# The decay of the first half of the channels in SBUF, its PSUM bank given to the ring

## The chip, the cores and the metric

One Trainium2 chip, one core of it. The metric is device microseconds of one execution, as the median of several. The kernel is written out by hand for the five engines: TensorE (PE, with its weight loads as PEld), VectorE (DVE), ScalarE (ACT), GpSimd (POOL) and the queue of SyncE (SP) that issues the DMAs.

## What is computed

Two transformer layers with adaptive layer norms over x of 8 batches x 512 positions x 128 channels. Only the first stage of the first layer matters here. It mixes each batch twice, from the same normed input:

```python
# causal attention, 16 heads of 8 channels
scores = jnp.where(causal, einsum('bqhd,bkhd->bhqk', q, k) * hd ** (-0.5), -inf)
attn_out = einsum('bhqk,bkhd->bqhd', softmax(scores), v).reshape(B, L, Dm) @ o_w + o_b
# selective state space model, 256 channels (two halves of 128), 16 states
def step(h, inp):
    xt, dtt, Bt, Ct = inp
    h = jnp.exp(dtt[..., None] * A) * h + (xt * dtt)[..., None] * Bt[:, None, :]
    y = einsum('bn,bdn->bd', Ct, h)
x = x + alpha * attn_out + (1.0 - alpha) * ssm_out
```

Behind it come an ffn, a mixture of eight experts with a shared one, banded attention and a last gated layer.

## The kernel before, in words

A planner (`plan_mixers` and its like) writes one list of steps. Each engine's program goes through this list in order and does its own share of each step, so the order of the instructions of every engine is fixed when the kernel is built. Between engines stand semaphore waits (`wait_ge`). Each engine works its queue in order: an instruction that waits holds all that is behind it.

The first stage runs from about 120 us to 840 us of the span. Three strands are woven together by `run_together`: `attend` (scores, exponential, weighing of the values), `maxima` (the row maxima of the scores, two units ahead) and `mamba` (the state space model), in fixed proportions. The stage repeats itself for each of the 8 batches, about every 93 us.

The state space model goes over 128 groups g (8 batches x 16 states). A group has two halves h of 128 channels, and takes:

- `spread` (L1863, SP): a DMA that spreads one row of B over 128 partitions into Bb, four groups ahead.
- `weight` (L1760, POOL): dBx = dtx * Bb, two instructions, two groups ahead. The buffer dBx holds four groups.
- `decay` (L1628, ACT): exp(A * dt), two instructions. Half 0 is written to PSUM bank 4, half 1 to bank 5. There is one buffer for each half, so the decay of group g+1 waits until the scan of group g has read it.
- `scan` (L1325, DVE): h = decay * h + dBx along the 512 positions, two instructions. Each reads the decay (PSUM) and dBx (SBUF) and writes hst (part of the tile hy, SBUF).
- `accumulate` (L1177 PE, L1261 DVE, in some groups ACT L1635 and POOL L1765): one group behind.

PSUM has 8 banks. In this stage bank 3 collects the weighed values, banks 4 and 5 hold the decay, and the five banks 0, 1, 2, 6 and 7 are the `ring`. Every other product of TensorE takes a bank of the ring by `take()`, which calls `first_free`: it picks the bank that the planner's own estimates have free first. So do the maxima (PE L1050, read by DVE L1315 into Mx), the scores (PE L1050, read by ACT L1569 into PT, then cut to the causal part by POOL L1740), the transposed states of `accumulate`, the projections and the branches of the model. TensorE's step waits for the release of its bank by the engine that read it last (`free[f"b{k}"]`).

The tile On is 128 x 2 x 512 in SBUF. POOL writes the normalised attention of head group 1 into On[:, 0] and of group 3 into On[:, 1] (`on`, L1745), and TensorE reads it four pieces of attention later (`wo`, line 1130). At the very start of the kernel On[:, 0] also serves as scratch (gtmp), and the mixture of experts later uses rows 0 to 32 of it (hr).

Of the kernel before, what the change touches and what calls it, by code (L numbers as in the profile page):

```python
# [10 lines left out]
ALU = mybir.AluOpType  # L11
ACT = mybir.ActivationFunctionType
# [152 lines left out]
def plan_mixers(p, r_h, r_n, lnb):  # L165

    free, up, step = p.free, p.up, p.step
    ring = [0, 1, 2, 6, 7]
    r_parts, r_v, r_qk, r_mr = {}, {}, {}, {}
    h_last = [None] * NB  # L170
    late, later, pts = [], [], [0]
# [65 lines left out]
    def normalise(b, g, m):  # L237
        hf, k = g // 2, 3
        it = step("os", b=b, g=g, m=m, os_free=free.get("Os"))
        it["o"] = free[f"b{k}"] = up("act_os")  # L240
        o1 = it["o"]
        yield
        yield
        k = take()
        it = step("on", b=b, g=g, o1=o1, bank=k, free=free.get(f"b{k}"), lrs_free=free.get(f"lrs{hf}"), on_free=free.get(f"On{hf}"))
        it["m"] = up("pe_dn")
        it["e1"] = free[f"b{k}"] = up("act_dn")
        it["e2"] = up("act_dn")
        it["o"] = free["Os"] = free[f"lrs{hf}"] = on = up("pool_on")
        for _ in range(4):  # L250
            yield
        k = take()
        it = step("wo", b=b, g=g, bank=k, free=free.get(f"b{k}"), on=on, h=h_last[b] or r_n[b])
        it["m"] = free[f"On{hf}"] = up("pe_wo")
        it["hd"] = free.get("hd")
        it["x"] = free[f"b{k}"] = up("act_hd")
        it["y"] = free["hd"] = h_last[b] = up("pool_h")
# [109 lines left out]

    def decay(g):
        b, n = divmod(g, 16)
        it = step("decay", g=g, dt=ssm[b]["dt"], free=[free.get(f"b{4 + h}") for h in range(2)])  # L370
        it["x"] = ssm[b]["decay", n] = [up("act_da"), up("act_da")]
        if n == 15:
            free[f"dtv{b % 2}"] = it["x"][1]

    def scan(g):
        b, n = divmod(g, 16)
        it = step("scan", g=g, into=ssm[b]["in", n], decay=ssm[b]["decay", n], free=[free.get(f"hst{2 * (g % 3) + h}") for h in range(2)])
        it["x"] = ssm[b]["h", n] = [up("dve_scan"), up("dve_scan")]
        for h in range(2):
            free[f"b{4 + h}"] = free[f"dBx{g % 4}{h}"] = it["x"][h]  # L380

    def accumulate(g):
        b, n = divmod(g, 16)
# [101 lines left out]
    mixer = mamba()  # L485
    drain(project(0))
    fetch(0)
    for k in (0, 1, 2):
        ring.remove(k)
    run_together(p.norms(first_norms([(1, 1)] + [(b, l) for l in range(2) for b in range(2, NB)])), 12, (mixer, 5, False))  # L490
    ring.extend((0, 1, 2))
    fetch(1)
    run_together(maxima(0), 23, (chain(values_of(0), project(1)), 8, True), (mixer, OFF, False))
    tops = chain(*[maxima(u) for u in range(1, NU)])
# [354 lines left out]
def build(nc, d, out):  # L849
    with ExitStack() as ctx:  # L850
# [38 lines left out]
        cT = sb("cT", [P, 16])  # L889
        mod = sb("mod", [P, 2, 6, NB])  # L890
        gab = sb("gab", [P, 4, NB])
        gtmp = On[:, 0, 0:96].rearrange("p (i j b) -> p i j b", i=3, j=4)
        avec = sb("avec", [P, 4])
        lsq = sb("lsq", [P, 2, T])
# [151 lines left out]
        def tensor_program(engine):  # L1046
# [22 lines left out]
            for kind, it in p.steps:  # L1069
# [57 lines left out]
                    mm(o[:], seld[:], Os[:]).then_inc(sems["pe_dn"], 1)  # L1127
                elif kind == "wo":
                    q.wait_ge(("ld_wo", 128), it["on"], it["free"])
                    mm(o[:], wo[:, it["g"] // 2, :], On[:, it["g"] // 2, :]).then_inc(sems["pe_wo"], 1)  # L1130
                elif kind == "taps":
                    q.wait_ge(("ld_in", 16), it["free"])
                    for h in range(2):
# [123 lines left out]
        def vector_program(engine):  # L1257
# [37 lines left out]
            for kind, it in p.steps:  # L1295
# [25 lines left out]
                elif kind == "scan":  # L1321
                    g = it["g"]
                    for h in range(2):
                        q.wait_ge(it["into"][h], it["decay"][h], it["free"][h])
                        engine.tensor_tensor_scan(hst[:, 2 * (g % 3) + h, :], bank[4 + h][:], dBx[:, g % 4, h, :], 0.0,  # L1325
                                                  ALU.mult, ALU.add).then_inc(sems["dve_scan"], 1)
                elif kind == "acc" and it["g"] % 16 and not it["beside"]:
                    b, n = divmod(it["g"], 16)
# [186 lines left out]
        def scalar_program(engine):  # L1515
# [25 lines left out]
            for kind, it in p.steps:  # L1541
# [82 lines left out]
                elif kind == "decay":  # L1624
                    b, n = divmod(it["g"], 16)
                    for h in range(2):
                        q.wait_ge(("dve_set", dve_set["A"]), it["dt"][h], it["free"][h])
                        engine.activation(bank[4 + h][:], dtv[:, b % 2, h, :], ACT.Exp,  # L1628
                                          scale=alog[:, h, n:n + 1]).then_inc(sems["act_da"], 1)
                elif kind == "acc" and (it["g"] % 16 == 0 or it["beside"]):  # L1630
                    b, n = divmod(it["g"], 16)
# [56 lines left out]
        def gpsimd_program(engine):  # L1688
# [39 lines left out]
            for kind, it in p.steps:  # L1728
# [13 lines left out]
                elif kind == "on":  # L1742
                    hf = it["g"] // 2
                    q.wait_ge(it["e2"], it["on_free"])
                    engine.tensor_tensor(On[:, hf, :], Os[:], rdn[:, hf, :], ALU.mult).then_inc(sems["pool_on"], 1)  # L1745
                elif kind in ("wo", "so"):
                    t = hT[:, it["b"], :]
                    q.wait_ge(it["x"], it["h"])
                    engine.tensor_tensor(t, t, hd[:], ALU.add).then_inc(sems["pool_h"], 1)
                elif kind == "dt":  # L1750
                    h, s = it["h"], it["b"] % 2
                    q.wait_ge(it["a3"], it["v1"], it["dtv_free"])
                    engine.tensor_tensor(dtv[:, s, h, :], sp1[:, h, :], sp2[:, h, :], ALU.add).then_inc(sems["pool_dt"], 1)
                    q.wait_ge(it["v2"], it["dtx_free"])
                    engine.tensor_tensor(dtx[:, s, h, :], dtv[:, s, h, :], xc[:, s, h, :], ALU.mult).then_inc(sems["pool_dt"], 1)
                elif kind == "weight":
                    b, sl = it["g"] // 16, it["g"] % 4
                    for h in range(2):
                        q.wait_ge(it["dx"][h], it["row"], it["free"][h])
                        engine.tensor_tensor(dBx[:, sl, h], dtx[:, b % 2, h], Bb[:, sl], ALU.mult).then_inc(sems["pool_dbx"], 1)  # L1760
                elif kind == "acc" and it["beside"]:
                    j = 2 * it["half"]
                    t = yT[:, j:j + 2, :]
                    q.wait_ge(it["y"], it["y_last"])
                    engine.tensor_tensor(t, t, yB[:, j:j + 2, :], ALU.add).then_inc(sems["pool_y"], 1)  # L1765
                elif kind == "yt":
                    h, s = it["h"], it["b"] % 2
                    q.wait_ge(it["y2"], it["z"])
                    engine.tensor_tensor(zg[:, s, h, :], zg[:, s, h, :], xc[:, s, h, :], ALU.mult).then_inc(sems["pool_yz"], 1)
                elif kind == "wsplit":  # L1770
                    e, s1, s2 = it["e"], stage[:, 2 * (it["i"] % 3), :], stage[:, 2 * (it["i"] % 3) + 1, :].rearrange("p (k n) -> p k n", k=4)
                    q.wait_ge(it["x1"])
                    engine.tensor_tensor(we1l[:, e, :], s1, we1h[:, e, :].bitcast(F32), ALU.subtract).then_inc(sems["pool_ws"], 1)
                    q.wait_ge(it["x2"])
                    engine.tensor_tensor(we2l[:, e], s2, we2h[:, e].bitcast(F32), ALU.subtract).then_inc(sems["pool_ws"], 1)
                elif kind == "moe_const":
                    q.wait_ge(it["done"])
                    engine.iota(iot_i[:], pattern=[[-1, 8]], base=8, channel_multiplier=0).then_inc(sems["pool_mc"], 1)
                    q.wait_ge(("pool_mc", 1))
                    engine.tensor_copy(iot[:], iot_i[:]).then_inc(sems["pool_mc"], 1)  # L1780
                elif kind == "moe_end":
                    t = acc[:, it["b"] % 2, :]
                    q.wait_ge(it["x"], it["acc"])
                    engine.tensor_tensor(t, t, prd[:, it["e"] % 2, :], ALU.add).then_inc(sems["pool_acc"], 1)  # L1784
                elif kind == "sc4" and it["s"] not in ON_DVE:
                    r, s = it["rg"], it["s"]
                    q.wait_ge(it["ready"], it["free"], it["done"])
                    engine.tensor_tensor(prod[:, it["ps"]], qkv[:, r % 3, 0, s:s + 1, :].broadcast_to([P, 8, P]), qkv[:, r % 3, 1],  # L1788
                                         ALU.mult).then_inc(sems["pool_p4"], 1)
                elif kind == "w4" and it["s"] not in ON_DVE:  # L1790
                    r, s = it["rg"], it["s"]
                    pr4 = scs[:, r % 2, :, 8 * s:8 * s + 8].rearrange("p k (h o) -> p k h o", o=1).broadcast_to([P, 8, 8, 16])
                    q.wait_ge(it["y"], it["free"])
                    engine.tensor_tensor(prod[:, it["ps"]].rearrange("p k (h x) -> p k h x", x=16), pr4,  # L1794
                                         qkv[:, r % 3, 2].rearrange("p k (h x) -> p k h x", x=16), ALU.mult).then_inc(sems["pool_w4"], 1)
                elif kind == "keys5":
                    t = kk[:, it["b"] % 2, :]
                    q.wait_ge(it["k"])
                    engine.tensor_tensor(t, t, t, ALU.mult).then_inc(sems["pool_k5"], 1)
# [150 lines left out]
```

## Time and profile before

| what | value |
| --- | --- |
| median of 3 runs | 1673.72 us (1668.92 to 1680.34) |
| the profiled execution, its own time | 1669.76 us |
| span of its profile, first to last instruction | 1668.0 us |
| granted TensorE clock, mean over the span | 0.934 |
| DVE busy | 1261.6 us (76% of the span) |
| PE busy | 1408.5 us (84%) |
| ACT busy | 1093.5 us (66%) |
| POOL busy | 863.4 us (52%) |

The profile counts an instruction as busy from its start to its end, and the end can contain time in which it was held inside the engine. Idle time is put down to the semaphore event that ended it. The shares are means over the whole span, and the first stage differs from the rest.

### The profile page before, as it was taken

How to read it: one execution, taken by the hardware profiler on the slowest of the kernel's cores; microseconds unless marked ns; L12 is line 12 of the kernel's file. 1: busy time of each engine (PE TensorE's matmuls, PEld its weight loads, DVE VectorE, ACT ScalarE, POOL GpSimd, SP SyncE). 2: the span in 40 equal slices, each digit the busy share in tenths (PEclk: the TensorE clock that was granted, in tenths of full speed). 3: DMA queues.
4: the chain of work that ended last, by engine and by line, in shares of the span. 5: the costliest groups of instructions: out<-in, count | busy, mean ns of one | idle time of the engine just before them, and what ended most of it. 6: DMA issues, size and time to landing. Idle time of an engine off the chain costs nothing. (4 is left out here: it accounts for less than half of the span.)

```text
span 1668.0 us, 22123 instructions
## 1 busy us (share of the span) xinstructions
PE 1408.5 (84%) x7164; PEld 884.0 (53%) x7164; DVE 1261.6 (76%) x1873; ACT 1093.5 (66%) x1864; POOL 863.4 (52%) x889
## 2 busy tenths in 40 slices
PE   3688898888989898887767887999999999868687
PEld 3234444444444444444324645787786877725573
DVE  2149999989798988989915858687686767848857
ACT  2475668686767778786746736777878788621017
POOL 3137677778696978878843113022222222248843
PEclk9787899999999999999988989999999999979889
DMA  3112222222222222222003010111111111000001
GB/s 90 45 39 83 77 63 78 80 75 70 64 68 67 78 73 68 80 76 75 27 1 95 19 48 26 33 48 45 40 49 39 45 45 45 26 0 1 0 1 50
DMA packets 61688, 84.73 MB, mean 51 GB/s; under 512 B 6621, under 2 KB 32071, under 8 KB 61575
## 3 DMA queue, kind: packets, MB, share of 16 engines
q1 hardware_dynamic: 61474, 83.30, 16.0%
q8 instruction: 58, 0.95, 0.2%
q14 instruction: 56, 0.45, 0.1%
q10 hardware_dynamic: 100, 0.03, 0.0%
HBM read 74.38 MB, written 8.78 MB: 50 GB/s over the span
## 5 line engine op out<-in xcount | busy, mean ns | idle before, releaser
L1760 POOL TENSOR_TENSOR dBx<-dtx,Bb 128x512 f32<-128x512 f32 x256 | 319.6, 1272 | 11.4 <-DMA Bb<-b_dram 10.1
L1355 DVE TENSOR_TENSOR hl<-lsq,hh 128x512 fp32r<-128x512 f32 x320 | 259.5, 821 | 86.7 <-ACT hh L1644 78.9
L1325 DVE TENSOR_TENSOR_SCAN hy<-bank,dBx 128x512 f32<-128x512 f32 x256 | 297.8, 1203 | 10.5 <-ACT bank L1628 6.0
L1641 ACT ACTIVATE lsq<-bank,vcol 128x512 f32<-128x512 f32 x320 | 219.4, 692 | 108.1 <-DVE hl L1355 61.0
L1050 PE MATMUL bank<-QK 127*128 127x128 bf16 (+7 forms) x1024 | 237.7, 318 | 46.6 <-DVE Mx L1315 27.9
L1315 DVE TENSOR_REDUCE Mx<-bank 128x1 f32<-128x384 f32 (+3 forms) x352 | 212.1, 627 | 57.5 <-PE bank L1050 56.7
L1784 POOL TENSOR_TENSOR stage<-stage,lrs 128x512 f32<-128x512 f32 x64 | 92.3, 1443 | 310.5 <-DVE lrs L1435 310.5
L1050 PE MATMUL bank<-x,we1h 128*128 128x512 f32 x640 | 210.7, 411 | 18.8 <-DVE x L1343 9.4
L1569 ACT ACTIVATE PT<-bank 128x512 f32<-128x512 f32 x320 | 183.7, 596 | 52.9 <-PE bank L1050 51.3
L1628 ACT ACTIVATE bank<-dtv,alog 128x512 f32<-128x512 f32 x256 | 170.4, 692 | 61.2 <-DVE hy L1325 60.8
L1050 PEld LDWEIGHTS bank<-QK 127*128 127x128 bf16 (+1 forms) x1024 | 94.3, 104 | 191.9 <-issue 51.5
L1261 DVE SCALAR_TENSOR_TENSOR hy<-bank,bc,hy 128x256 f32<-128x256 f32 x408 | 169.0, 474 | 9.1 <-PE bank L1177 6.3
L1644 ACT ACTIVATE hh<-bank,vcol 128x512 fp32r<-128x512 f32 x248 | 170.5, 688 | 0.0
L1740 POOL TENSOR_SCALAR_AFFINE_SELECT PT<-PT 128x256 f32<-128x256 f32 (+1 forms) x320 | 112.0, 362 | 100.9 <-ACT PT L1569 98.7
L1177 PE MATMUL bank<-ident,hy 128*128 128x128 f32 x1024 | 152.1, 291 | 12.2 <-DVE hy L1325 4.8
L1050 PEld LDWEIGHTS bank<-x,we1h 128*128 128x128 f32 x640 | 121.6, 194 | 59.1 <-DVE x L1343 13.5
L1177 PEld LDWEIGHTS bank<-ident,hy 128*128 128x128 f32 x1024 | 117.8, 148 | 49.0 <-issue 14.4
L1050 PE MATMUL bank<-hh,we2h 128*128 128x512 f32 x320 | 128.5, 402 | 7.7 <-DVE hl L1355 7.3
L1050 PE MATMUL bank<-x,we1l 128*128 128x512 f32 x320 | 128.1, 400 | 0.0
L1050 PE MATMUL bank<-hh,we2l 128*128 128x512 f32 x320 | 126.3, 395 | 0.0
L1050 PE MATMUL bank<-hl,we2h 128*128 128x512 f32 x320 | 126.3, 395 | 0.0
L1050 PE MATMUL bank<-PT,Vb 128*32 128x512 f32 (+7 forms) x1024 | 89.1, 443 | 16.4 <-POOL PT L1740 15.3
(258 smaller groups left out, 2393.6 us busy)
## 6 DMA issues: line engine op xcount, KB each, us to landing
Bb<-b_dram SPq DMA_DIRECT2D x128, 256.0 KB, 3.6
stage<-w_rows SPq DMA_DIRECT2D x64, 256.0 KB, 3.2
parts<-part SPq DMA_DIRECT2D x16, 384.0 KB, 2.7
QK<-parts SPq DMA_DIRECT2D x64, 96.0 KB
QK<-parts SPq DMA_DIRECT2D x64, 64.0 KB
stage<-in_L_ffn_We_dram SPq DMA_DIRECT2D x16, 256.0 KB, 3.3
hy<-in_L_attn_x_dram SPq DMA_DIRECT2D x8, 256.0 KB, 5.8
QK<-parts SPq DMA_DIRECT2D x64, 32.0 KB
```

Source lines behind the costliest of these rows:

```text
L1050: return engine.matmul(o, l, r, start=start, stop=stop, tile_position=pos, skip_group_check=True)
L1177: x = engine.transpose(o[:, 256 * jj + P * h:256 * jj + P * h + P], hst[:, a + h, P * j:P * j + P], ident[:])
L1261: return engine.scalar_tensor_tensor(out=o, in0=a, scalar=s, in1=b, op0=op0, op1=op1)
L1315: engine.tensor_reduce(Mx[:, it["u"] % 2, qi, h:h + n], o[:, 0:P * (qi + 1) * n].rearrange("p (i c) -> p i c", i=n), AX.X, ALU.max).then_i ...
L1325: engine.tensor_tensor_scan(hst[:, 2 * (g % 3) + h, :], bank[4 + h][:], dBx[:, g % 4, h, :], 0.0, ALU.mult, ALU.add).then_inc(sems["dve_sc ...
L1355: engine.tensor_tensor(hl[:, sl, :], full[:, f, :], hh[:, sl, :].bitcast(F32), ALU.subtract).then_inc(sems["dve_hl"], 1)
L1569: engine.activation(PT[:, it["sl"], :], o[:], ACT.Exp).then_inc(sems["act_exp"], 1)
L1628: engine.activation(bank[4 + h][:], dtv[:, b % 2, h, :], ACT.Exp, scale=alog[:, h, n:n + 1]).then_inc(sems["act_da"], 1)
L1641: engine.activation(full[:, f, :], o[:], fn, bias=bias).then_inc(sems["act_up"], 1)
L1644: engine.activation(hh[:, sl, :], o[:], fn, bias=bias).then_inc(sems["act_up"], 1)
L1740: engine.affine_select(out=t, in_=t, compare_op=ALU.is_ge, fill=0.0, base=0, pattern=[[0, 2], [1, P]] if o2 else [[1, P]], channel_multipl ...
L1760: engine.tensor_tensor(dBx[:, sl, h], dtx[:, b % 2, h], Bb[:, sl], ALU.mult).then_inc(sems["pool_dbx"], 1)
```

## The change

The decay of half 0 goes to SBUF, into the half of On that head group 3 used (`dec = On[:, 1, :]`). Both head groups now write On[:, 0], so that `on` waits for the last `wo`, whatever its group. Bank 4 is released and becomes the sixth bank of the ring, from the start of the stage on (it is taken out of the ring for the first norms, which use it, and put back after them). The decay of half 1 stays in bank 5. No instruction is added or taken away, and the order of each engine's instructions is the same.

```diff
 def plan_mixers(p, r_h, r_n, lnb):
-    ring = [0, 1, 2, 6, 7]
+    ring = [0, 1, 2, 4, 6, 7]
...
-        it = step("on", b=b, g=g, o1=o1, bank=k, free=free.get(f"b{k}"), lrs_free=free.get(f"lrs{hf}"), on_free=free.get(f"On{hf}"))
+        it = step("on", b=b, g=g, o1=o1, bank=k, free=free.get(f"b{k}"), lrs_free=free.get(f"lrs{hf}"), on_free=free.get("On"))
...
-        it["m"] = free[f"On{hf}"] = up("pe_wo")
+        it["m"] = free["On"] = up("pe_wo")
...
     def decay(g):
         b, n = divmod(g, 16)
-        it = step("decay", g=g, dt=ssm[b]["dt"], free=[free.get(f"b{4 + h}") for h in range(2)])
+        it = step("decay", g=g, dt=ssm[b]["dt"], free=(free.get("dec"), free.get("b5")))
...
         for h in range(2):
-            free[f"b{4 + h}"] = free[f"dBx{g % 4}{h}"] = it["x"][h]
+            free[("dec", "b5")[h]] = free[f"dBx{g % 4}{h}"] = it["x"][h]
...
-    for k in (0, 1, 2):
+    for k in (0, 1, 2, 4):
         ring.remove(k)
     run_together(p.norms(first_norms([(1, 1)] + [(b, l) for l in range(2) for b in range(2, NB)])), 12, (mixer, 5, False))
-    ring.extend((0, 1, 2))
+    ring.extend((0, 1, 2, 4))
...
         gab = sb("gab", [P, 4, NB])
+        dec = On[:, 1, :]
...
-                    mm(o[:], wo[:, it["g"] // 2, :], On[:, it["g"] // 2, :]).then_inc(sems["pe_wo"], 1)
+                    mm(o[:], wo[:, it["g"] // 2, :], On[:, 0, :]).then_inc(sems["pe_wo"], 1)
...
-                        engine.tensor_tensor_scan(hst[:, 2 * (g % 3) + h, :], bank[4 + h][:], dBx[:, g % 4, h, :], 0.0,
+                        engine.tensor_tensor_scan(hst[:, 2 * (g % 3) + h, :], bank[5][:] if h else dec, dBx[:, g % 4, h, :], 0.0,
...
-                        engine.activation(bank[4 + h][:], dtv[:, b % 2, h, :], ACT.Exp,
+                        engine.activation(bank[5][:] if h else dec, dtv[:, b % 2, h, :], ACT.Exp,
...
-                    engine.tensor_tensor(On[:, hf, :], Os[:], rdn[:, hf, :], ALU.mult).then_inc(sems["pool_on"], 1)
+                    engine.tensor_tensor(On[:, 0, :], Os[:], rdn[:, hf, :], ALU.mult).then_inc(sems["pool_on"], 1)
```

## Rows read from the trace of the kernel before

**Rows 1.** The page, busy times, and DVE's busy tenths in 40 slices.

```profile
PE 1408.5 (84%) x7164; PEld 884.0 (53%) x7164; DVE 1261.6 (76%) x1873; ACT 1093.5 (66%) x1864; POOL 863.4 (52%) x889
...
DVE  2149999989798988989915858687686767848857
```

**Rows 2.** Stretches view, the first stage: stretch, its length, busy time by engine, clock, DMA.

```profile
120.00:840.00 720.00, 609.68 (x3877) 328.58 (x3877) 652.18 (x1020) 520.43 (x909) 555.12 (x666) 0.95 0.22 70
```

**Rows 3.** The same view, one batch in four quarters (PE, PEld, DVE, ACT, POOL, clock).

```profile
475.00:498.00 23.00, 18.58 (x125) 11.78 (x126) 22.83 (x37) 12.70 (x23) 20.36 (x27) 0.85 0.19 55
498.00:521.00 23.00, 21.18 (x125) 10.37 (x124) 20.15 (x32) 17.53 (x32) 19.00 (x24) 1.00 0.27 90
521.00:545.00 24.00, 21.82 (x146) 12.09 (x146) 17.96 (x28) 19.58 (x33) 13.73 (x17) 1.00 0.17 55
545.00:568.00 23.00, 20.35 (x132) 10.61 (x131) 21.17 (x35) 20.74 (x39) 21.11 (x25) 0.93 0.28 89
```

**Rows 4.** Waits from 120 to 840 us: total in us, times, the longest in us.

```profile
POOL PT L1740 <- ACT PT L1569: 94.7, 57, 5.9
ACT bank L1628 <- DVE hy L1325: 60.8, 75, 3.2
...
PEld bank L1050 <- DVE Mx L1315: 48.6, 59, 2.7
DVE Mx L1315 <- PE bank L1050: 47.1, 35, 3.2
...
PEld bank L1050 <- POOL PT L1740: 19.0, 26, 2.0
...
DVE hy L1325 <- POOL dBx L1760: 4.5, 1, 4.5
```

**Rows 5.** Timeline of the first stage near 408 us: start, duration, then the instruction.

```profile
407.65 2.49 POOL L1760 TENSOR_TENSOR dBx<-dtx,Bb 128x512 f32<-128x512 f32 x2
...
408.08 2.33 DVE L1325 TENSOR_TENSOR_SCAN hy<-bank,dBx 128x512 f32<-128x512 f32 x2
```

**Rows 6.** Timeline of DVE in a later stage, near 1088 us.

```profile
1088.18 1.66 DVE L1343 TENSOR_TENSOR x<-nT,x 128x512 fp32r<-128x512 f32 x1
```

**Rows 7.** Timeline of POOL over the same microseconds.

```profile
1087.89 1.40 POOL L1784 TENSOR_TENSOR stage<-stage,lrs 128x512 f32<-128x512 f32 x1 [3.60 <-DVE lrs L1435]
```

**Rows 8.** Line views of L1470, L1435 and L1775: duration in ns, min/median/max.

```profile
L1470 DVE TENSOR_TENSOR scs<-scs,mx x4: 691/692/694, 1489.9 to 1590.0; 128x512 f32<-128x512 f32 x4
...
L1435 DVE TENSOR_TENSOR lrs<-bank,stage x64: 680/683/692, 1081.7 to 1453.5; 128x512 f32<-128x512 f32 x64
...
L1775 POOL TENSOR_TENSOR we2l<-stage,we2h x10: 1279/1727/1742, 899.2 to 1039.2; 128x512 fp32r<-128x512 f32 x10
```

**Rows 9.** Groups by shape of POOL, 120 to 840 us: count, busy us, mean ns, idle before.

```profile
L1760 POOL TENSOR_TENSOR dBx<-dtx,Bb 128x512 f32<-128x512 f32 x256 | 319.6, 1272 | 11.4 <-DMA Bb<-b_dram 10.1 <-DVE hy L1325 1.4
L1740 POOL TENSOR_SCALAR_AFFINE_SELECT PT<-PT 128x256 f32<-128x256 f32 x175 | 70.2, 407 | 78.6 <-ACT PT L1569 77.2
L1765 POOL TENSOR_TENSOR hy<-hy,nT 128x512 f32<-128x512 f32 x36 | 44.9, 1269 | 21.3 <-ACT nT L1635 21.3
L1740 POOL TENSOR_SCALAR_AFFINE_SELECT PT<-PT 128x128 f32<-128x128 f32 x120 | 33.4, 295 | 17.6 <-ACT PT L1569 17.5
...
L1769 POOL TENSOR_TENSOR zg<-zg,xc 128x512 f32<-128x512 f32 x14 | 17.6, 1276 | 14.1 <-DVE xc L1261 14.1
```

**Rows 10.** The page, costliest groups: the scan and the maxima on DVE.

```profile
L1325 DVE TENSOR_TENSOR_SCAN hy<-bank,dBx 128x512 f32<-128x512 f32 x256 | 297.8, 1203 | 10.5 <-ACT bank L1628 6.0
...
L1315 DVE TENSOR_REDUCE Mx<-bank 128x1 f32<-128x384 f32 (+3 forms) x352 | 212.1, 627 | 57.5 <-PE bank L1050 56.7
```

**Rows 11.** Line views of L1628 and L1678 on ACT: duration in ns, min/median/max.

```profile
L1628 ACT ACTIVATE bank<-dtv,alog x256: 672/692/747, 120.1 to 832.3; 128x512 f32<-128x512 f32 x128
...
L1678 ACT ACTIVATE fl<-hT,vcol x16: 705/710/714, 1633.7 to 1655.6; 128x512 f32<-128x512 f32 x16
```

**Rows 12.** Line view of L1745, the writes of On.

```profile
L1745 POOL TENSOR_TENSOR On<-Os,lrs x16: 1257/1270/1277, 225.6 to 872.3; 128x512 f32<-128x512 f32 x16
```

## The prediction

> **What bounds the kernel now.** I read the page first. Over the span PE is busiest, but DVE's tenths stand at 8 and 9 in nearly every slice from the fourth to the twentieth and fall after it [rows 1]: the part that the change touches is a stage with a limit of its own. The stretches view then gives that stage: of 720 us DVE is busy 652 (91%), PE 610, POOL 555, ACT 520 [rows 2]. So DVE leads and has 68 us of idle time left, and nobody else is far behind.
>
> The same view by quarters of one batch shows that the limit moves [rows 3]. In the first quarter DVE is busy 22.8 of 23 us: it alone sets the time. In the second and third it has 2.9 and 6.0 us idle, while PE is busy 21.2 of 23 and 21.8 of 24: PE sets the time there (the branches of the next batch). In the fourth DVE has 1.8 us idle, with POOL at 21.1 and ACT at 20.7 beside it. The waits view agrees: DVE waits for PE's maxima 47.1 us in 35 pieces, and PE's weight loads wait for DVE's maxima 48.6 us in 59 [rows 4]. Both waits go through banks of the ring, each in its own quarters.
>
> The last thing to see is POOL beside the scans. At 407.65 POOL starts its two dBx, and at 408.08 DVE starts its two scans. They run through each other in 2.49 and 2.33 us, which is two times what one of each takes, 1.27 and 1.20 [rows 5, 9, 10]. Today a scan has one input in PSUM and one in SBUF, and it is not disturbed.
>
> **The change, part by part.** All sums are made against the profiled execution, 1669.8 us, which lies 3.9 us under the median of 1673.7.
>
> *Half 0's scan with two inputs in SBUF: the wait on DVE.* The trace has no such scan, but it has other DVE operations with two fp32 inputs in SBUF beside a busy POOL. Left alone, 128x512 of it takes 692 ns (L1470) [rows 8]. At 1088.18 the like operation took 1660 ns: POOL had started at 1087.89 for 1.40 us, so that 1.11 us of it were left, and 1.11 + 0.55 is 1.66 [rows 6, 7]. DVE thus stood still until POOL was done, less 0.14 us that overlap. I apply this to the scan. How much of a POOL instruction is left when a scan of half 0 starts? POOL ran 256 dBx of 1.272 us, 175 selects of 0.407, 120 of 0.295, and 115 others (666 in all) of 1.27 us, L1765 and L1769 the first and last of them [rows 2, 9]. A start at a random moment meets on average (256 x 1.272² + 175 x 0.407² + 120 x 0.295² + 115 x 1.27²) / (2 x 720) = 0.44 us of rest. It meets a busy POOL in 77% of cases (555 of 720), which takes off 0.77 x 0.14 = 0.11. That leaves 0.33 us a scan, and 128 of them give 42 us. The pair near 408 us would have paid more (2 x 1.27 from 407.65: 0.84 us left of the first, so 0.7), others pay nothing. The bounds: nothing, if a scan, which spends 1203 ns where the plain operation spends 692, leaves POOL enough room [rows 8, 10]; and 1.27 - 0.14 = 1.13 us each, 145 us, if every scan met a dBx at its start. I take 42.
>
> The Trainium skill (SBUF — State Buffer, Who interferes with whom) has this as a rule: a DVE instruction with two SBUF inputs and a GpSimd instruction that reads SBUF exclude each other, and the second to issue blocks until the first is finished. By the letter of it the wait is the full 0.44, or 57 us in all. The trace agrees on the order, and takes 0.14 off each.
>
> How much of the 42 lies beside other work? A quarter of a batch has four such scans, 1.3 us. The first quarter has no cover and pays 1.3. The fourth pays the same, since its idle 1.8 us are single waits and not a reserve. The second pays half of it, the third a quarter, for PE leads there [rows 3]. That is 3.6 us a batch length of 93, and 720 / 93 = 7.7 of them: 28 us.
>
> *The same exclusion on POOL.* A POOL instruction that comes while the scan reads is held: L1775 takes 1279 ns alone and 1727 in most cases [rows 8], beside two such DVE operations. A scan that waited starts as POOL's instruction ends, and the next POOL instruction, usually the second dBx, then waits 1.20 - 0.14 = 1.06 us. I put this at half the scans, and at 0.4 us for most of the others: 0.7 us a group on average, 90 us in all. The bounds are 0 and 128 x 1.06 = 136. POOL's idle time (165 us of 720) covers the sum but not each quarter: with 2.8 us more the four quarters have 23.2, 21.8, 16.5 and 23.9 us of POOL work, and the first and fourth, lengthened to 24.3 by DVE, are then full. Queued behind the held dBx are the selects on PT, for which PE waits 19.0 us now; dBx itself is two groups early and was waited for once [rows 4]. For late selects I charge 0.8 us in each of these two quarters, 12 us in all. What it costs if that cover is gone stands among the rivals.
>
> *The wait on ACT.* The decay of the next group waits for half 0's scan to end, already 75 times for 60.8 us [rows 4], and behind it in ACT's queue stand the exponentials of the scores. The scan now ends up to 1.1 us later. ACT is busy 72% of the stage, so I charge nothing beyond the quarters above.
>
> *Where the decay lies.* ACT's write: into PSUM 692 ns; the nearest row from SBUF to SBUF with a column as scale 710 [rows 11]. 18 ns x 128 = 2 us on ACT, beside other work; I take 1. DVE's read: a two-input operation with one input in PSUM takes 683 ns, with both in SBUF and POOL quiet 692 [rows 8]; 9 ns x 128 = 1 us. The Trainium skill (VectorE: DVE Perf Modes, the section on the TRN2 errata) gives a fixed part of 120 cycles from PSUM and 58 from SBUF. By that each scan would be 65 ns shorter, an estimate of 8 us gained. The rows above do not show it.
>
> *A sixth bank.* It can only shorten waits. It lets PE be one product further ahead when a PE-led quarter begins, so each of DVE's 35 waits for maxima can shrink by about one maximum, 0.63 us [rows 4, 10]: 22 us at most. PE's own waits for DVE get shorter too, but in DVE-led quarters that moves no end. Not every bank goes to a maximum, and not each wait follows a full ring, so I take 10. The bounds are 0 and 22.
>
> *On with one half.* 16 writes in 647 us [rows 12], one every 40 us, and the read follows four pieces of attention later, some 10 us. No wait: 0. Bank 4 stays out of the ring while the first norms use it: 0. No DMA moves. The stages behind 840 us are unchanged.
>
> Sum: 28 + 12 + 1 + 1 - 10 = +32 us. 1669.8 + 32 = 1702, and on the scale of the median 1673.7 + 32 = **1706 us**.
>
> **The rivals.**
>
> *The bank wins (ends on the other side).* The scan takes two cycles' worth of time per element, and if DVE's reads then fit between POOL's, the 42 us and the 90 us are both nothing. The full 22 us of the ring stay, less 2: 1654 us. For it: no row shows a scan beside POOL with two SBUF inputs, and the plain operation is not a scan. Against it: in rows 6 and 7 DVE did not slow down, it stood still, which is not a matter of rate. The point from which it decides is a wait of 22 / 128 = 0.17 us a scan, if all of it reached the path. The page on SBUF has no exception for slower operations.
>
> *Absorbed.* DVE waits, but its 68 idle us, most of them waits for PE and POOL, take it up, and POOL shifts so that it starts after the scan rather than before it: a third of the charge stays, +13, against -10 for the ring. About 1677 us. For it: PE leads half of the quarters. Against it: 22.83 of 23 us in the first quarter.
>
> *POOL becomes the bound.* If POOL is ready behind every scan, it loses the full 136 us and has 691 of 720 us to do, with 95 us of waits for ACT's exponentials that do not all vanish [rows 4]. Selects come late, PE waits with the weighing, its clock falls (it was granted 0.85 in the quarter where PE was busy least [rows 3]), and the stage takes about 785 us: +65, 1739 us. For it: POOL at 20.4 and 21.1 of 23 us. Against it: the quarters led by PE give time back.
>
> **How the numbers follow.** My forecast 0.55, the bound on POOL 0.16, absorbed 0.19, the bank wins 0.10. The range goes from 1680, a little above the case where the idle time takes it up, to 1742, just above POOL's case. A measurement of this kernel can tell about 1% from no change, 17 us: faster than 1657 holds 0.07 (most of the bank's case), within 1% 0.22 (absorbed, and the rest of the bank's), slower than 1690 holds 0.71.
>
> **What would show it.** L1325 falls into two groups. The one that reads bank stays at 1203 ns. The one that reads On has a median well above 1203, near 1.5 us in the mean and up to 2.3. L1760, now 1272 in the mean with hardly any spread, gets a mean of 1.4 or more and a maximum near 2.3. DVE's waits for maxima fall from 47 to about 37 us. ACT's waits for L1325 grow. The stages behind the first keep their length. A mean of 1.21 us for the scans that read On would prove the first three terms wrong at once; a stage that has grown by over 50 us would say that POOL's share was too small.

## The result, and the profile after

The changed kernel takes 1696.8 us in the median of 4 runs (1694.5 to 1702.2), against 1671.8 for the kernel before. The ratio is 1.0146, with an interval of 1.0100 to 1.0192: slower by 17 to 32 us, 24 in the middle. 1706 was forecast, with 1680 to 1742 as the range. The profiled execution is the longest of the four, 1702.2 us.

The page of the changed kernel gives the first reading. These are its busy times, DVE's and POOL's tenths in 40 slices, and the groups (count, busy us, mean ns, idle before) that answer to [rows 1, 9, 10]. The change adds one line near the head of the file, so L1325 is now L1326, and so on.

```profile
PE 1431.9 (84%) x7164; PEld 899.0 (53%) x7164; DVE 1310.9 (77%) x1873; ACT 1093.8 (64%) x1864; POOL 960.6 (56%) x889
...
DVE  2139998989898998989943858688686777748866
...
POOL 3138687989898998989953212022222222238842
...
L1761 POOL TENSOR_TENSOR dBx<-dtx,Bb 128x512 f32<-128x512 f32 x256 | 355.9, 1412 | 8.3 <-DMA Bb<-b_dram 7.1
...
L1326 DVE TENSOR_TENSOR_SCAN hy<-On,dBx 128x512 f32<-128x512 f32 x128 | 199.3, 1557 | 17.2 <-ACT On L1629 11.0
L1741 POOL TENSOR_SCALAR_AFFINE_SELECT PT<-PT 128x256 f32<-128x256 f32 (+1 forms) x320 | 167.0, 539 | 54.3 <-ACT PT L1570 53.7
...
L1326 DVE TENSOR_TENSOR_SCAN hy<-bank,dBx 128x512 f32<-128x512 f32 x128 | 152.6, 1192 | 0.0
```

DVE is busy 49 us longer than before and POOL 97 us, with the same instructions. The scans have split in two. The 128 (half 1) that read the bank take 1192 ns, the 128 (half 0) that read On take 1557. On POOL the dBx went from 1272 to 1412 ns, and the 320 selects from 362 ns to 539. POOL was busy 77% of the first stage before [rows 2]; now its tenths stand at 8 and 9 through nearly the whole stage, like DVE's.

The line views of the changed kernel (duration in ns, min/median/max) show the spread, which a mean hides: the scan from On is not slow in itself, it is 1204 ns at best and 2324 at worst. The dBx has a median of 1272, as before, and a tail to 2302.

```profile
L1326 DVE TENSOR_TENSOR_SCAN hy<-On,dBx x128: 1204/1502/2324, 126.3 to 860.4; 128x512 f32<-128x512 f32 x128
...
L1761 POOL TENSOR_TENSOR dBx<-dtx,Bb x256: 1254/1272/2302, 125.1 to 851.5; 128x512 f32<-128x512 f32 x128
...
L1629 ACT ACTIVATE On<-dtv,alog x128: 709/722/772, 122.6 to 857.8; 128x512 f32<-128x512 f32 x128
```

Where the lengths come from can be seen in the timeline. First that of DVE (start in us, duration, instruction).

```profile
501.61 1.87 DVE L1326 TENSOR_TENSOR_SCAN hy<-On,dBx 128x512 f32<-128x512 f32 x1
503.40 1.19 DVE L1326 TENSOR_TENSOR_SCAN hy<-bank,dBx 128x512 f32<-128x512 f32 x1
...
505.69 1.21 DVE L1326 TENSOR_TENSOR_SCAN hy<-On,dBx 128x512 f32<-128x512 f32 x1
```

And that of POOL over the same microseconds.

```profile
501.12 3.42 POOL L1770 TENSOR_TENSOR zg<-zg,xc 128x512 f32<-128x512 f32 x2 [0.24 <-DVE xc L1262]
504.50 3.46 POOL L1761 TENSOR_TENSOR dBx<-dtx,Bb 128x512 f32<-128x512 f32 x2
```

At 501.61 the scan met a POOL instruction of 1.27 us that had begun at 501.12: 0.78 us were left, and the scan took 1.87, which is 1.20 + 0.78 - 0.11. POOL's second instruction then had to wait, and the pair took 3.42 us where two alone take 2.5. At 505.69 it was the other way round: the scan started as the first of two dBx was ending, kept its 1.21 us, and POOL's pair took 3.46. Either engine can be the one that stands.

The single scan is no exception. The starts and ends of all 128 scans from On were set beside POOL's in the same trace. A scan took 1.20 us and what was left of POOL's running instruction at its start, less 0.12 us, and nine in ten lie within 0.02 us of this. The 29 that met an idle POOL took 1.21 us, as half 0's scans did before. One started 0.02 us after a dBx, which then took 2.30 us while the scan kept its 1.21: here the dBx was the one held.

The waits of the changed kernel from 120 to 860 us (total in us, times, longest), to be read beside [rows 4]:

```profile
ACT On L1629 <- DVE hy L1326: 67.2, 43, 4.2
...
POOL PT L1741 <- ACT PT L1570: 45.9, 24, 6.2
PEld bank L1051 <- POOL PT L1741: 33.9, 35, 3.3
...
DVE Mx L1316 <- PE bank L1051: 28.5, 35, 2.2
...
PE bank L1051 <- POOL PT L1741: 24.6, 22, 3.0
...
ACT bank L1629 <- DVE hy L1326: 19.1, 50, 0.4
```

DVE's waits for maxima fell from 47.1 to 28.5 us: the sixth bank works. POOL's idle time before selects halved (94.7 to 45.9), for it is now held elsewhere, and PE's weight loads wait for selects 33.9 us in place of 19.0.

The starts of the scans in the trace give the stage batch by batch, each from its first scan to that of the next, the last to the end of its last scan. The first batch went from 78.3 to 84.2 us, the six in the middle from 557.1 to 569.1 together, 2.0 each, and the last from 77.5 to 83.2. That is 5.9 + 12.0 + 5.7 = 23.6 us, as much as the medians differ (24). The other 8 to 9 us by which the two profiled spans differ lie before and behind the stage. These are the stretches from the first hl (L1355, then L1356) to the end, before and after, in the stretches view (length, busy times by engine, clock, DMA):

```profile
904.30:1668.00 763.70, 677.13 (x2860) 496.62 (x2859) 560.85 (x776) 477.27 (x797) 248.84 (x143) 0.94 0.11 33
```

```profile
930.50:1700.40 769.90, 696.09 (x2860) 503.52 (x2859) 567.36 (x776) 477.65 (x797) 245.25 (x143) 0.91 0.11 32
```

The instructions are the same, the granted clock is lower and PE is busy longer. Of the kernels below, the one built on the kernel before has 764 us there, the others, built on the changed kernel, 766 to 770. So a small effect behind the stage is not excluded by the profiles. It does not show in the medians of the two kernels that take the change apart: in `ring5_sbuf` and `ring6_psum` the stage alone, +37.5 and -14.1 us, gives what their ratios give, 38 and -14.

### The profile page after: what moved, and what is told of

Its sections match the earlier page's. It is cut to its first block and busy times, and to the rows that moved or that the text cites. A ratio compares the mean times of both kernels' runs of the same rounds, so it can differ in the third digit from the quotient of the medians.

```text
span 1700.4 us, 22126 instructions
## 1 busy us (share of the span) xinstructions
PE 1431.9 (84%) x7164; PEld 899.0 (53%) x7164; DVE 1310.9 (77%) x1873; ACT 1093.8 (64%) x1864; POOL 960.6 (56%) x889
## 5 line engine op out<-in xcount | busy, mean ns | idle before, releaser
L1761 POOL TENSOR_TENSOR dBx<-dtx,Bb 128x512 f32<-128x512 f32 x256 | 355.9, 1412 | 8.3 <-DMA Bb<-b_dram 7.1
L1356 DVE TENSOR_TENSOR hl<-lsq,hh 128x512 fp32r<-128x512 f32 x320 | 263.8, 836 | 79.6 <-ACT hh L1645 71.0
L1785 POOL TENSOR_TENSOR stage<-stage,lrs 128x512 f32<-128x512 f32 x64 | 88.7, 1386 | 314.2 <-DVE lrs L1436 314.2
L1326 DVE TENSOR_TENSOR_SCAN hy<-On,dBx 128x512 f32<-128x512 f32 x128 | 199.3, 1557 | 17.2 <-ACT On L1629 11.0
L1741 POOL TENSOR_SCALAR_AFFINE_SELECT PT<-PT 128x256 f32<-128x256 f32 (+1 forms) x320 | 167.0, 539 | 54.3 <-ACT PT L1570 53.7
L1326 DVE TENSOR_TENSOR_SCAN hy<-bank,dBx 128x512 f32<-128x512 f32 x128 | 152.6, 1192 | 0.0
L1178 PEld LDWEIGHTS bank<-ident,hy 128*128 128x128 f32 x1024 | 122.7, 151 | 47.9 <-issue 15.0
L1629 ACT ACTIVATE On<-dtv,alog 128x512 f32<-128x512 f32 x128 | 92.8, 725 | 67.3 <-DVE hy L1326 67.2
```

The costliest lines, as they stand in the source:

```text
L1178: x = engine.transpose(o[:, 256 * jj + P * h:256 * jj + P * h + P], hst[:, a + h, P * j:P * j + P], ident[:])
L1326: engine.tensor_tensor_scan(hst[:, 2 * (g % 3) + h, :], bank[5][:] if h else dec, dBx[:, g % 4, h, :], 0.0, ALU.mult, ALU.add).then_inc(se ...
L1356: engine.tensor_tensor(hl[:, sl, :], full[:, f, :], hh[:, sl, :].bitcast(F32), ALU.subtract).then_inc(sems["dve_hl"], 1)
L1629: engine.activation(bank[5][:] if h else dec, dtv[:, b % 2, h, :], ACT.Exp, scale=alog[:, h, n:n + 1]).then_inc(sems["act_da"], 1)
L1741: engine.affine_select(out=t, in_=t, compare_op=ALU.is_ge, fill=0.0, base=0, pattern=[[0, 2], [1, P]] if o2 else [[1, P]], channel_multipl ...
```

## The experiments

Each kernel was run four to six times, beside eleven runs of the kernel before. Line numbers are shifted by a few between the kernels. Waits are those from 120 us to the end of the first stage.

**The two edits apart.** `ring5_sbuf` keeps the decay in SBUF and gives the bank back:

```diff
-    ring = [0, 1, 2, 4, 6, 7]
+    ring = [0, 1, 2, 6, 7]
```

(with the same bank left out of the lists around the first norms). Diffs are against the changed kernel and are excerpts, unless something else is said.

> The changed kernel with the ring left at five banks (bank 4 unused): the decay of half 0 in SBUF alone. Theory (exclusion between a two-input scan and POOL costs, the bank pays a part back): scans that read On stay at a mean of 1.5 to 1.6 us, POOL's dBx at 1.4 us, DVE's waits for maxima return from 28 us toward 47 us, and the time is 1707 us (1.02 of the kernel before). Rival (the bank gives nothing, the whole difference is the exclusion): the same 1697 us as the changed kernel.

Measured: 1712.0 us, ratio 1.0227 (1.0203 to 1.0252). `ring6_psum` keeps the bank and takes the second SBUF input away:

```diff
-                        q.wait_ge(it["into"][h], it["decay"][h], it["free"][h])
-                        engine.tensor_tensor_scan(hst[:, 2 * (g % 3) + h, :], bank[5][:] if h else dec, dBx[:, g % 4, h, :], 0.0,
+                        q.wait_ge(it["into"][h], it["decay"], it["free"][h])
+                        engine.tensor_tensor_scan(hst[:, 2 * (g % 3) + h, :], bank[5][:], dBx[:, g % 4, h, :], 0.0,
```

> The changed kernel with both halves' scans reading the decay in bank 5; the decay of half 0 is still written to On by ACT but read by nobody, so half 0 is computed with half 1's decay. Ring of six. Theory: without a second SBUF input the scans are all 1.19 to 1.21 us, POOL's dBx 1.27 us, and what is left is the sixth bank alone: 1660 us (0.993 of the kernel before). Rival (the loss is not the exclusion but ACT's write to SBUF, or the order of the banks): it stays at 1690 us or more with scans at 1.2 us.

Measured: 1662.9 us, ratio 0.9917 (0.9893 to 0.9940). In this kernel half 0 uses half 1's decay, so that its result is not the one wanted, and its scan waits for both decays: DVE stands 19.8 us before scans for ACT, where it was 6.0 in the kernel before. The 14 us of the bank may thus be a little too few.

With the kernel before and the changed kernel these make a square:

| ratio to before | ring of five | ring of six |
| --- | --- | --- |
| no scan with two SBUF inputs | 1 | 0.9917 |
| half 0's scans with two | 1.0227 | 1.0146 |

The second SBUF input costs 38 us in the left column (0.0227 x 1672) and 38 us in the right (1.0146 / 0.9917 is 1.0231). The bank gives 14 us in each row. The interval of 1.0146 is half a per cent either way, so 38 and 14 in the right column and the lower row are good to some 8 us. Within that the two effects add up, and the theories of both runs held. The scans say the same. This is the line view of L1326 in `ring6_psum`:

```profile
L1326 DVE TENSOR_TENSOR_SCAN hy<-bank,dBx x256: 1196/1210/1225, 125.6 to 823.5; 128x512 f32<-128x512 f32 x128
```

its wait for maxima:

```profile
DVE Mx L1316 <- PE bank L1051: 30.6, 31, 2.2
```

and in `ring5_sbuf` the group of the scans from On:

```profile
L1326 DVE TENSOR_TENSOR_SCAN hy<-On,dBx 128x512 f32<-128x512 f32 x128 | 193.5, 1512 | 10.9 <-ACT On L1629 6.4 <-POOL dBx L1761 4.5
```

with its wait for maxima:

```profile
DVE Mx L1316 <- PE bank L1051: 46.2, 36, 3.2
```

The waits for maxima go with the ring (46.2 and 47.1 us at five banks, 28.5 and 30.6 at six), and the length of the scans goes with the second SBUF input. ACT still writes half 0's decay to SBUF in `ring6_psum`, so this write, at 722 ns in place of 692, is not what costs.

**Which scan of the pair.** `swap_halves` puts half 1's decay in On and half 0's in bank 4, with bank 5 in the ring:

```diff
-                        engine.tensor_tensor_scan(hst[:, 2 * (g % 3) + h, :], bank[5][:] if h else dec, dBx[:, g % 4, h, :], 0.0,
+                        engine.tensor_tensor_scan(hst[:, 2 * (g % 3) + h, :], dec if h else bank[4][:], dBx[:, g % 4, h, :], 0.0,
```

(with the decay's write, its waits and the ring changed to match).

> Half 1's decay in On and half 0's in bank 4, bank 5 in the ring: the second scan of each pair has the two SBUF inputs. Theory (the wait is what is left of the POOL instruction that runs when the scan starts): in the trace of the kernel before, POOL has 0.62 us left on average when the scan of half 1 starts and 0.42 us when that of half 0 does, so the slowed scans take 1.7 us in the mean and the time is 1708 us. Rival (a fixed price of two SBUF inputs, or a share of the port): 1.56 us and 1697 us again.

Measured: 1720.6 us, ratio 1.0269 (1.0246 to 1.0292). The group of the slowed scans, and under it the wait of PE's weight loads for selects:

```profile
L1326 DVE TENSOR_TENSOR_SCAN hy<-On,dBx 128x512 f32<-128x512 f32 x128 | 214.1, 1672 | 0.0
```

```profile
PEld bank L1051 <- POOL PT L1741: 42.5, 28, 3.3
```

The scans came out as the theory had them, 1.67 us for 1.7, so the price of a scan does depend on what POOL has left at that moment and is not a fixed one. The time is 12 us above the expectation: the theory counted DVE alone, and PE's waits for selects rose too, from 33.9 us in the changed kernel.

**What POOL is doing then.** `weight_later` moves the two dBx in POOL's order:

```diff
-                for ahead, f in ((4, spread), (2, weight)):
-                    if g + ahead < 16 * NB:
-                        f(g + ahead)
+                if g + 4 < 16 * NB:
+                    spread(g + 4)
...
                 accumulate(g - BEHIND)
+            if g + 2 < 16 * NB:
+                weight(g + 2)
+            if g >= BEHIND:
                 next(beside, None)
```

> The changed kernel with POOL's two dBx of group g+2 issued after the accumulation step, half a group later in POOL's order. Theory (which POOL instruction a scan meets sets its wait): the scans of half 0 meet selects of 0.3 to 0.4 us more often than dBx of 1.27 us, their mean falls from 1.56 to about 1.4 us, and the time falls to 1685 us. Rival (POOL and the scan exclude each other whatever the order, and what DVE wins POOL loses): scan means change but the time stays at 1697 us within 5.

Measured: 1720.7 us, ratio 1.0267 (1.0242 to 1.0292), 20 us above the changed kernel. Both expectations missed. The mean of the scans did not change at all, and the waits for selects doubled:

```profile
L1328 DVE TENSOR_TENSOR_SCAN hy<-On,dBx 128x512 f32<-128x512 f32 x128 | 199.5, 1558 | 23.1 <-ACT On L1631 13.0 <-POOL dBx L1763 10.1
```

```profile
PEld bank L1053 <- POOL PT L1743: 70.9, 42, 6.7
...
PE bank L1053 <- POOL PT L1743: 57.8, 28, 6.4
```

The theory failed at its first step. The dBx of group g+2 began 2.5 us after half 0's scan of group g ended, in the median, where it had been 1.0. That is 1.5 us later and not half a group (2.9), and 71 scans now met a dBx, where 56 had, and 14 a select, where 19 had. A select that stands behind a late dBx comes late itself: PE's two kinds of waits for selects are 71 and 58 us, where they were 34 and 25, and DVE's waits for maxima rose from 28.5 to 43.8 us. DVE's own waits for dBx are 10 us. It is more for the selects than for the dBx that somebody waits.

**Shorter POOL instructions.** `split_dbx` cuts each dBx in two:

```diff
-                        engine.tensor_tensor(dBx[:, sl, h], dtx[:, b % 2, h], Bb[:, sl], ALU.mult).then_inc(sems["pool_dbx"], 1)
+                        engine.tensor_tensor(dBx[:, sl, h, 0:256], dtx[:, b % 2, h, 0:256], Bb[:, sl, 0:256], ALU.mult)
+                        engine.tensor_tensor(dBx[:, sl, h, 256:T], dtx[:, b % 2, h, 256:T], Bb[:, sl, 256:T], ALU.mult).then_inc(sems["pool_dbx"], 1)
```

> The changed kernel with each dBx of POOL cut into two instructions of 256 columns, one behind the other. Theory (a scan waits for what is left of the one POOL instruction that runs): the pieces take about 0.65 us, the mean rest at a random start falls from 0.44 to 0.31 us, scans that read On come down from 1.56 to about 1.43 us, and the time to 1688 us, though POOL is busy some 13 us longer. Rival (the two engines exclude each other for the sum of their reading, whatever the pieces): scans and time stay at 1.56 us and 1697 us or above.

Measured: 1718.3 us, ratio 1.0274 (1.0239 to 1.0308). Its group of scans, the line view of the second piece, and the waits for selects:

```profile
L1326 DVE TENSOR_TENSOR_SCAN hy<-On,dBx 128x512 f32<-128x512 f32 x128 | 188.4, 1472 | 16.4 <-ACT On L1629 11.8 <-POOL dBx L1762 4.6
```

```profile
L1762 POOL TENSOR_TENSOR dBx<-dtx,Bb x256: 714/728/1693, 124.9 to 872.6; 128x256 f32<-128x256 f32 x128
```

```profile
PEld bank L1051 <- POOL PT L1741: 54.2, 34, 4.6
...
PE bank L1051 <- POOL PT L1741: 45.3, 26, 4.3
```

The scans got shorter, 1557 to 1472 ns, as the theory said they would (it had 1430). The time went the wrong way. A half of 256 columns takes 728 ns and not 650. Two of them take 184 ns more than one whole, which is 47 us more on POOL, where 13 had been assumed. PE's waits for selects grew again (from 34 and 25 us). The scans gained 11 us and the kernel lost 22. That POOL's longer work and the selects behind it are the reason is read from these rows and was not tested apart.

**Who waits.** `gated_dbx` has POOL wait for the scan of half 0 before it starts the dBx two groups ahead:

```diff
-        it = step("weight", g=g, dx=ssm[b]["dx"], row=ssm[b]["row", n], free=[free.get(f"dBx{sl}{h}") for h in range(2)])
+        it = step("weight", g=g, dx=ssm[b]["dx"], row=ssm[b]["row", n], free=[(free.get(f"dBx{sl}{h}"), ("dve_scan", 2 * g - 3) if g > 1 else None) for h in range(2)])
```

(with `weight` called behind `scan`).

> The changed kernel in which POOL's dBx of group g+2 also waits for the scan of half 0 of group g, the one with two SBUF inputs. It shifts the wait from DVE to POOL. Theory (the loss of the changed kernel is DVE's waiting): scans that read On now rarely meet a dBx, their mean falls from 1.56 to about 1.3 us, and the time to 1680 us. Rival (POOL is as much the bound as DVE, and what counts is the time in which neither may read): POOL idles before dBx, PE waits longer for the selects behind it (more than the 34 us of weight loads in the changed kernel), and the time is 1697 us or above.

Measured: 1692.1 us, ratio 1.0115 (1.0095 to 1.0136). The middle is 5 us below the changed kernel, but the intervals overlap: a gain is possible and not shown. The means tell why so little moved: the scans went from 1557 to 1542 ns only. POOL waited at the gate 12 times for 25.4 us. In the changed kernel 56 scans met a dBx, and 49 of these belonged to the scan's own group or the next one, which the gate lets pass. It could keep away only the other 7. In `gated_dbx` 52 scans met one, all of those two groups. The group and the wait:

```profile
L1327 DVE TENSOR_TENSOR_SCAN hy<-On,dBx 128x512 f32<-128x512 f32 x128 | 197.4, 1542 | 15.8 <-ACT On L1630 11.3 <-POOL dBx L1762 4.5
```

```profile
POOL dBx L1762 <- DVE hy L1327: 25.4, 12, 3.1
```

**What a bank is worth.** `ring4_psum` is the kernel before with bank 2 out of the ring:

```diff
-    ring = [0, 1, 2, 6, 7]
+    ring = [0, 1, 6, 7]
```

(and out of the lists around the first norms).

> The kernel before with bank 2 taken out of the ring: four banks, both decays in PSUM. It tells what a bank of the ring is worth. Theory (each bank shortens DVE's waits for maxima, the first ones more): DVE waits for maxima rise from 47 to 70 us or more and the time is 1700 us. Rival (every bank is worth the same 14 us): 1687 us. Rival (five were enough, and the gain from the sixth has another source): within 3 us of the kernel before.

Measured: 1718.5 us, ratio 1.0279 (1.0252 to 1.0306). Its waits for maxima:

```profile
DVE Mx L1315 <- PE bank L1050: 81.7, 55, 7.1
```

The fifth bank is worth 47 us and the sixth 14, and DVE's waits for maxima go 82, 47, 31 with four, five and six banks. The first theory held in kind; it had the fifth bank at 28 us.

**Six banks with the complete computation and no second SBUF input.** `one_bank` passes both halves' decays through bank 5, one after the other, and draws the two scans apart:

```diff
-                scan(g)
+                scan(g, 0)
+                decay(g, 1)
                 next(beside, None)
                 next(behind, None)
                 yield
+                scan(g, 1)
                 if g + 1 < 16 * NB:
-                    decay(g + 1)
+                    decay(g + 1, 0)
```

> Both halves' decays pass one after the other through bank 5 in fp32, in the order decay 0, scan 0, decay 1, other work, scan 1, decay 0 of the next group, accumulation of the group before; ring of six, nothing in On. The computation is complete. Theory (the sixth bank is worth 14 us where no scan has two SBUF inputs): scans take 1.2 us, and with some waits of DVE for ACT between the halves the time is 1668 us, below the kernel before. Rival (the exponential cannot be had in time between the halves): DVE waits for ACT 0.3 us or more a scan, 40 us in all, and the time is 1700 us.

Measured: 1738.0 us, ratio 1.0383 (1.0354 to 1.0411). Its waits:

```profile
ACT bank L1630 <- DVE hy L1327: 234.6, 186, 4.1
...
DVE Mx L1318 <- PE bank L1053: 75.5, 40, 5.1
DVE hy L1327 <- ACT bank L1630: 44.0, 91, 3.0
...
PEld bank L1053 <- ACT PT L1571: 40.8, 79, 1.9
```

The rival came near with DVE's wait (44 us for 40), but not with the time, which is 38 us above its 1700. The larger part seems to be ACT's. It stands 235 us before the decays, and the exponentials of the scores queue behind them: PE's weight loads wait 41 us for them, POOL 138 us, where it was 46 in the changed kernel. The banks that they read come free late, and DVE waits 75.5 us for maxima in spite of six banks. `one_bank_spread` tried to cure this by one half of the accumulation between each decay and its scan. Against `one_bank`:

```diff
-                scan(g, 0)
-                decay(g, 1)
+                decay(g, 0)
+                if g >= BEHIND:
+                    accumulate(g - BEHIND, (0,))
+                scan(g, 0)
...
-                scan(g, 1)
-                if g + 1 < 16 * NB:
-                    decay(g + 1, 0)
+                decay(g, 1)
+                if g >= BEHIND:
+                    accumulate(g - BEHIND, (1,))
+                scan(g, 1)
...
-                accumulate(g - BEHIND)
```

> As one_bank, but each half's decay is issued with one half of the accumulation between it and its scan, so that ACT's exponential and its wait for the scan before have about 1.9 us of DVE's work to lie beside. The computation is complete and nothing lies in On. Theory (one_bank lost its gain in ACT's queue, where the exponentials of the scores stand behind 231 us of waits for scans): ACT's waits for scans fall below 150 us, DVE's below 20, and the time is 1680 us or less. Rival (one buffer for two halves costs too much in any order): 1710 us or more.

Measured: 1765.5 us, ratio 1.0560 (1.0540 to 1.0580). Its waits:

```profile
PE bank L1184 <- DVE hy L1331: 136.8, 99, 6.2
ACT bank L1634 <- DVE hy L1331: 136.2, 139, 4.3
...
DVE hy L1331 <- ACT bank L1634: 61.9, 66, 5.3
```

ACT's waits did fall to 136 us, below the 150 of the theory, but DVE's rose to 62 in place of falling below 20, and a new one came: the transposes of a group now stand close behind its second scan, and PE waits for it 137 us. The rival's time, 1710 us or more, was right. That no order of one buffer can pay, as the rival says, is not shown by two of them.

## Why the prediction was right, step by step

- *The scan waits for what POOL has left, less a small overlap.* Right, in kind and size. 0.33 us a scan and 42 us in all were worked out; the scans from On take 199.3 - 128 x 1.203 = 45 us more, 0.35 us each, and the rule holds scan by scan. `swap_halves` and `split_dbx` moved this term up and down as it says. That a scan, slow as it is, might let POOL through is refuted. Luck had a part in the size: the prediction took a start at a random moment, which gives 0.33 us for either half, and half 1's scans paid 1.67 - 1.20 = 0.47 us in `swap_halves`. In the trace of the kernel before, POOL has 0.43 us left in the mean when half 0's scan starts and 0.62 us when half 1's does. Half 0 happens to lie near the random value.
- *The same on POOL, 90 us.* The sum is right, 97 us, its make-up is not. The prediction had half the scans hold an instruction for 1.06 us and most others for 0.4, and spoke of the second dBx as the usual one to be held. In the trace of the changed kernel 116 POOL instructions start while one of the 128 scans from On runs, 66 of them selects and 38 dBx, and 97 / 116 is 0.84 us each. The dBx are held for 36 us and the short selects for 55 (the busy times of their groups in the two pages). That the sum came within 7 us is in part luck.
- *What of it reaches the end: 28 us by DVE and 12 by late selects.* Right in the sum: 38 us in both columns of the square. Its spread over the batches was not as even as the prediction had made it. In the kernel before DVE is busy 77.6 of the first batch's 78.3 us and 77.3 of the last one's 77.5, so that nothing covers a longer scan there. These two batches lost 7.4 and 5.7 us in `ring5_sbuf`, the full 16 x 0.35 = 5.6 us or more, and the six in the middle 4.1 each (557.1 to 581.5), where 40 / 7.7 = 5.2 had been worked out. How the 38 divide between DVE and the selects was not separated.
- *A sixth bank, 10 of at most 22 us.* The term that was mis-sized most: 14 us, and waits for maxima 17 to 19 us down where 10 were expected. With this the sum is 42 - 14 = 28 in place of 32, and 24 were measured.
- *ACT's write and DVE's read.* ACT's write costs 30 ns in the median in place of 18, hidden as forecast. The read from SBUF costs nothing that can be seen: the shortest scan from On is 1204 ns, and half 0's shortest was 1205 before. The 65 ns that the scan would have gained, by the estimate from the Trainium skill (VectorE: DVE Perf Modes, the section on the TRN2 errata), are not there either.
- *ACT's waits for the scans grow.* Right: 60.8 to 86.3 us.
- *The rivals.* "The bank wins" fell with the first item. It took the bank for 20 us, where `ring6_psum` gives 14. "Absorbed" had a third of the charge stay. In `ring5_sbuf` 4.1 of 5.6 us a batch stayed in the middle and all of it in the outer two, so it is false. The 2.0 us that a middle batch loses in the changed kernel are what the bank leaves of the charge. "POOL becomes the bound" did not come true in the changed kernel, but `weight_later` and `split_dbx` show how near it is: 20 us and more for a change on POOL that left the mean of DVE's scans alone or made it shorter.

The scan with two SBUF inputs and POOL's instructions exclude each other in both directions, but for an overlap of some 0.11 to 0.14 us. The Trainium skill (SBUF — State Buffer, Who interferes with whom) has the rule that the second to issue blocks until the first is finished. The trace agrees, for tensor_tensor_scan too, but for that overlap.

What stays open: a version with six banks, the complete computation and no scan with two SBUF inputs that is faster than the kernel before. `ring6_psum` shows that there would be 14 us to be had, and the two ways tried here lost more in ACT's and PE's queues.

## What to carry to other kernels

Before a DVE operand is moved from PSUM to SBUF, look at its other operand and at POOL: if the other one is in SBUF and POOL is busy with SBUF, each such instruction waits for what is left of POOL's, and POOL for it, and the mean rest can be estimated beforehand from counts and durations (sum of n x L² over twice the stage). The starts in the trace of the kernel before give it better: the formula had 0.33 us for both halves, and 0.35 and 0.47 were measured. Of two engines that exclude each other, the one with idle time can still be the costly one, by what is queued behind the held instruction. What a PSUM bank in a ring is worth shows roughly in the leader's waits on that ring. Here the fifth bank took 35 us off these waits and 47 off the time, the sixth 17 and 14.

## What the runs showed that had not been expected

- POOL's tensor_tensor of 128x256 takes 728 ns and that of 128x512 takes 1272. If the time grows evenly with the columns, the fixed part is 184 ns (2 x 728 - 1272), where some 50 ns had been assumed.
- One bank of the ring taken away costs more (47 us) than the second SBUF input of 128 scans (38 us).
- Moving the dBx half a group later in POOL's list moved them 1.5 us, not 2.9, and onto more scans (71 for 56). The scans kept their mean, 1558 ns, and the kernel lost 20 us, with PE's waits for the selects behind the dBx doubled.
